# The value product of an attention kernel from fp32 to fp16 parts, with a new order of the copies around it

## The reference

```python
qh, kh, vh = split_heads(q @ Wq), split_heads(k @ Wk), split_heads(v @ Wv)
dots = einsum('bhid,bhjd->bhij', qh, kh) * SCALE          # then mask and causal mask
attn = softmax(dots)
out = einsum('bhij,bhjd->bhid', attn, vh)                 # the value product
x = x + tanh(g_xattn) * (out_as_rows @ Wo + bo)
```

## Time and profile before

| | before |
|---|---|
| median of 3 runs | 1624.48 us (1622.92 to 1630.77) |
| the profiled execution | 1626.47 us |
| its span, first to last instruction | 1624.6 us |
| busy share: PE, PEld, DVE, ACT, POOL | 94%, 77%, 85%, 77%, 64% |

### The profile page before, as it was taken

One profiled execution on the slowest core, in us unless ns is written; L12 is line 12 of the kernel. 1 busy time (PEld: TensorE's weight loads), 2 busy tenths in 40 slices (PEclk: granted clock), 3 DMA queues, 4 the chain that ended last, 5 costly groups with the idle time before them and its releaser, 6 DMA issues. The chain is left out here.

```text
span 1624.6 us, 38058 instructions
## 1 busy us (share of the span) xinstructions
PE 1530.6 (94%) x12556; PEld 1251.8 (77%) x12556; DVE 1385.1 (85%) x2247; ACT 1253.4 (77%) x3222; POOL 1033.8 (64%) x1004
## 2 busy tenths in 40 slices
PE   7899999999999999999999999789989997995998
PEld 5787887877877878878778788677767776775887
DVE  7888888888888888888888889878887998998996
ACT  5887887888778778878887787566758998885674
POOL 3988988888888889888888888600006664740000
PEclk9999999999999999999999999999998999997999
DMA  6554445444444544454444445369957884755664
GB/s 195 118 127 103 105 106 122 104 92 115 106 105 103 126 102 105 107 121 104 92 115 106 105 103 98 86 205 344 321 215 262 282 287 153 276 227 187 218 214 145
DMA packets 347365, 252.23 MB, mean 155 GB/s; under 512 B 287792, under 2 KB 317616, under 8 KB 344368
## 3 DMA queue, kind: packets, MB, share of 16 engines
q1 hardware_dynamic: 347312, 251.58, 55.1%
HBM read 105.25 MB, written 76.02 MB: 112 GB/s over the span
## 5 line engine op out<-in xcount | busy, mean ns | idle before, releaser
L496 ACT ACTIVATE prob<-masked,neg_max 128x128 f32<-128x128 f32 x1024 | 397.6, 391 | 35.1 <-DVE neg_max L662 31.6
L431 POOL TENSOR_TENSOR prob_parts<-prob,prob_parts 128x512 f16<-128x512 f32 x254 | 310.3, 1241 | 2.7 <-ACT prob_parts L504 1.6
L426 POOL TENSOR_TENSOR prob<-prob,scaled 128x512 f32<-128x512 f32 x256 | 271.6, 1061 | 20.1
L660 DVE TENSOR_TENSOR masked<-score,mask_add 128x512 f32<-128x512 f32 x256 | 174.6, 682 | 74.0 <-PE score L963 67.9
L504 ACT ACTIVATE prob_parts<-prob 128x512 f16<-128x512 f32 x254 | 159.0, 627 | 75.6 <-POOL prob L426 71.7
L496 ACT ACTIVATION_READ_ACCUMULATOR prob<-masked,neg_max 128x1 f32 x1024 | 193.3, 189 | 0.0
L662 DVE TENSOR_REDUCE neg_max<-masked 128x4 f32<-128x512 f32 x256 | 175.6, 686 | 8.8
L438 POOL TENSOR_TENSOR probT<-turn 128x512 f32<-128x512 f16 x125 | 173.2, 1386 | 0.0
L1723 POOL TENSOR_SCALAR xThi<-n_x 128x1024 fp32r<-128x1024 int16 x15 | 43.8, 2919 | 202.9 <-DMA n_x<-n_x_d 166.8
L976 PE MATMUL y<-wo_hi,o_hi 128*128 128x256 f32 x508 | 148.3, 292 | 15.9 <-DVE o_lo L667 15.2
L424 POOL TENSOR_TENSOR scaled<-rsums,pscale 128x4 f32<-128x4 f32 x256 | 66.4, 259 | 124.0 <-DVE rsums L654 123.9
(11 more groups left out here) (249 smaller groups left out, 4485.5 us busy)
## 6 DMA issues: line engine op xcount, KB each, us to landing
gate<-gate_d SPq DMA_DIRECT2D x30, 768.0 KB, 4.3
n_x<-n_x_d SPq DMA_DIRECT2D x25, 512.0 KB, 4.9
gate_d<-stage SPq DMA_DIRECT2D x8, 1536.0 KB, 5.5
n_u_d<-w_raw SPq DMA_DIRECT2D x16, 768.0 KB, 4.1
stage<-n_u_d SPq DMA_DIRECT2D x16, 768.0 KB, 6.0
gate_d<-gate SPq DMA_DIRECT2D x7, 1536.0 KB, 5.5
x_in<-in_x SPq DMA_DIRECT2D x16, 512.0 KB, 3.9
ctx_in<-in_ctx_columns SPq DMA_DIRECT2D x16, 512.0 KB, 4.8
```

The lines of the kernel that those rows point to most:

```text
L426: gp.tensor_tensor(prob[:, h], prob[:, h], scaled[:, h, :].rearrange("p (b o) -> p b o", o=1).broadcast_to([P, NB, P]), ALU.mult).then_inc ...
L431: gp.tensor_tensor(prob_parts[:, h, 1], prob[:, h].rearrange("p b k -> p (b k)"), prob_parts[:, h, 0], ALU.subtract).then_inc(prob_low, 1)
L496: nc.scalar.activation(prob[:, h, b, :], masked[:, h, b, :], ACT.Exp, bias=neg_max[:, h, b:b + 1], accum_out=psums[:, h, b:b + 1]).then_in ...
L660: nc.vector.tensor_tensor(masked[:, h], score[h][:], mask_add[:], ALU.add).then_inc(masked_done, 1)
```

## The change

- `times_v` multiplies fp16 parts: the turned high and low halves in `turn` are read directly, and the values are kept as fp16 high and low halves (`v16`). Three fp16 matmuls (high by high, high by low, low by high) take the place of one fp32 matmul. Both joins and `probT` go; the transposing DMA waits for `pv_done` instead of the join.
- So that fp16 holds them, the values are scaled by a bound for each group: the largest entries of the context by column (`ctx_top`, VectorE) times the largest entries of `Wv` by row (`w_top`, VectorE, once), summed by four one-column matmuls (`value_bound`, TensorE, in unit 7 for the next group) and turned into a factor (`value_scale`). The residual multiplies by `y_unit`, which undoes it.
- Each value product is copied twice: `values_high` on ScalarE, behind the copy of the keys, then `values` on VectorE (scaled product minus high half), behind the second reciprocals.
- TensorE takes the (first) value product of a unit right behind the keys, ahead of the `Wo` product.
- ScalarE's `high_prob` of the second head moves from the end of a unit to the next unit, behind the copy of the queries.
- Smaller moves: `add_bias` on GpSimd to unit 1, `residual`, `second_max` and `normalise` to other places of VectorE's units; at the start, the scores of unit 0 ahead of the values, and `w_high_part(3)` and the tanh into unit 0; the last unit is turned through an fp16 split.

```diff
-            def join_prob(u, h, slot, times):
-                dve.wait_ge(prob_turned[h][slot], 16 * times)
-                wait(dve, pv_done, u)
-                nc.vector.tensor_tensor(probT[:, h], turn[:, slot, h, 0:NB], turn[:, slot, h, NB:2 * NB],
-                                        ALU.add).then_inc(probT_copied[h], 1)
...
             def turn_prob(u, h):
                 sp.wait_ge(prob_low, 2 * u + h + 1)
-                wait(sp, probT_copied[h], u - 1)
+                wait(sp, pv_done, u - 1)
...
+            def values_high(g, i, n):
+                b, before = nth(g, i)
+                if n == 0:
+                    act.wait_ge(v_scaled, 4 * g + 3)
+                act.wait_ge(projected[b], before + 1)
+                nc.scalar.activation(v16[:, n % NB, n // NB, 0], proj[b][:], ACT.Copy, scale=v_mul[:, 0:1]).then_inc(v_high, 1)
...
+                if not isinstance(g, int) or 2 <= u < U + 2:
+                    high_prob(u - 2, 1, (c + 1) % 2, NC // 2 * g + (c - 1) // 2)
+                early = isinstance(g, int) and g == 0 and c < 3
...
                 if soft:
                     exps(u - 1, 0)
-                if new:
+                if new and not early:
                     copy_k(g, c, u)
+                for i, n in vs[:1]:
+                    values_high(g, i, n)
...
-            def values(g, c):
-                for i, n in jobs_of(c, "v"):
+            def values(g, jobs):
+                for i, n in jobs:
                     b, before = nth(g, i)
-                    dve.wait_ge(projected[b], before + 1)
-                    nc.vector.tensor_copy(v_sb[:, n % NB, 0:VH], proj[b][:]).then_inc(copied[b], 1)
+                    dve.wait_ge(v_high, NC * g + n + 1)
+                    nc.vector.scalar_tensor_tensor(v16[:, n % NB, n // NB, 1], proj[b][:], v_mul[:, 0:1], v16[:, n % NB, n // NB, 0],
+                                                   ALU.mult, ALU.subtract).then_inc(copied[b], 1)
+
+            def ctx_top(g):
+                dve.wait_ge(ctx_loaded, 16 * (g + 1))
+                nc.vector.tensor_reduce(c_top[:], ctx_in[:], X, ALU.max, apply_absolute_value=True).then_inc(v_scaled, 1)
...
             w_low_part(2)
+            nc.vector.tensor_reduce(w_top[:, 0], staged(2), X, ALU.max, apply_absolute_value=True)
+            dve.wait_ge(w_loaded[5], 16)
+            nc.vector.tensor_reduce(w_top[:, 1], staged(5), X, ALU.max, apply_absolute_value=True)
+            ctx_top(0)
             w_low_part(3)
...
+                    for n, (m, t) in enumerate(((0, 0), (0, 1), (1, 0))):
+                        for h in range(2):
+                            at = c % NB * P + h * HD
+                            last = nc.tensor.matmul(pv[h * HD:(h + 1) * HD, b, :], v16[:, b, c // NB, m, at:at + HD],
+                                                    turn[:, slot, h, t * NB + b, :], start=(n == 0), stop=(n == 2))
                 last.then_inc(pv_done, 1)
+
+            def value_bound(g):
+                pe.wait_ge(v_scaled, 4 * g + 1)
+                for k in range(KC):
+                    for half in range(2):
+                        last = nc.tensor.matmul(trans[:, 0, 0:1], c_top[:, k:k + 1].broadcast_to([P, P]), w_top[:, half, k:k + 1],
+                                                start=(k == 0 and half == 0), stop=(k == KC - 1 and half == 1))
+                last.then_inc(v_bound, 1)
...
+                if new:
+                    for i, n in jobs_of(c, "v")[:1]:
+                        value(g, i, n)
                 if oldest:
...
                     out_product(u - 4, (c - 4) % NC)
                 if nxt:
                     transpose_in(g, *ts[1])
+                    value_bound(g + 1)
```

More of the change, by code:

```diff
@@ L449, in step @@
                         make_rstd2(g - 1)
[L450 to L453, removed]
+                if c == 1 and not (isinstance(g, int) and g == 0):
+                    add_bias(g - 1)
+                if c == 6 and new and not more:
+                    add_bias(g)
                 if soft:
@@ L532, in step @@
                     exps(u - 1, 1)
-                if isinstance(g, int) and g == 0 and c < 3:
+                if early and c < 2:
                     w_high_part(4 + c)
-                if new and c > 2:
-                    for i, n in jobs_of(c, "v"):
-                        b, before = nth(g, i)
-                        act.wait_ge(projected[b], before + 1)
-                        nc.scalar.activation(v_sb[:, n % NB, VH:2 * VH], proj[b][:], ACT.Copy).then_inc(copied[b], 1)
+                for i, n in vs[1:]:
+                    values_high(g, i, n)
                 if soft:
@@ L731, in step @@
                     second_norm(g - 1, NB // 2, NB)
-                if c == 6 and more:
-                    normalise(g + 1)
+                if c == 5 and more:
+                    normalise(g + 1, 0, NB // 2)
+                if c == 6 and after_first and more:
+                    second_max(g - 1)
+                if c == 3 and after_first:
+                    residual(g)
                 if isinstance(g, int):
@@ L847, in _ @@
             attended_low(U - 3)
-            for h in range(2):
-                join_prob(U - 2, h, 0, U // 2)
             attended_low(U - 2)
             weight_values(2, 1)
[L852 to L855, removed]
+            for h in range(2):
+                dve.wait_ge(v_high, NC * G + h + 1)
+                nc.vector.tensor_tensor(turn[:, 1, h, NB:2 * NB], trans[:], turn[:, 1, h, 0:NB], ALU.subtract).then_inc(last_turned, 1)
+                if h == 0:
+                    ffn_low_part(0)
             for n in range(1, 4):
@@ L937, in scores_free, with times_v @@
                     wait(pe, masked_done, 2 * (u - 1) + h + 1)
-            def times_v(u, c, then=None):
+            def times_v(u, c, slot, times, then=None):
                 for h in range(2):
-                    pe.wait_ge(probT_copied[h], u + 1)
+                    if times is None:
+                        pe.wait_ge(last_turned, 2)
+                    else:
+                        pe.wait_ge(prob_turned[h][slot], 16 * times)
                 wait(pe, out_split, u)
@@ L996, in step @@
                     weights_left(g, c, jobs_of(c, "k")[0][0], 1)
+                if first:
+                    scores_free(g, c, u)
+                    scores(g, c, u)
+                    value_bound(0)
                 if nxt:
                     transpose_in(g, *ts[0])
+                if first or fourth:
+                    pe.wait_ge(w_ready, 3 if first else 6)
+                if new:
+                    for i, n in jobs_of(c, "v")[:1]:
+                        value(g, i, n)
                 if oldest:
@@ L1006, in step @@
                     transpose_in(g, *ts[1])
-                if first or fourth:
-                    pe.wait_ge(w_ready, 3 if first else 6)
+                    value_bound(g + 1)
                 if new:
-                    for i, n in jobs_of(c, "v"):
+                    for i, n in jobs_of(c, "v")[1:]:
                         value(g, i, n)
                 if old:
-                    times_v(u - 3, co, (g, c, u) if new else None)
-                if new:
+                    times_v(u - 3, co, (c + 1) % 2, NC // 2 * g + (c - 1) // 2, (g, c, u) if new else None)
+                if new and not first:
                     if not old:
```

122 lines of the change are left out of this document (71 added, 51 removed).

## The result

The changed kernel takes 1682.26 us (median of 4 runs, 1680.25 to 1685.06) against 1624.67 beside it: 1.034 times as long, interval 1.032 to 1.036. 1602 was forecast, with a range of 1586 to 1634. The profiled execution has a span of 1681.8 us, against 1624.6.

What follows compares the result with a forecast made beforehand. TensorE was taken to set the pace, 7.98 us a unit. Value product -24, order -23, value_bound +14, new stalls +6 and start +4.5 sum to -22.5 us: 1602 us from a 1624.48 median, range 1586 to 1634.

Steps and rivals of the forecast that it cites:

- The value product: TensorE's probabilities times values in fp16: 0.83 us instead of 1.03, 0.20 gained a unit, -24 us in all.
- Rival 2: Loads set the step of TensorE's value product, which then takes 1.17 us: 1644 us in all; chance 0.08.
- The order on TensorE: Value product ahead of the Wo product, second high half later on ScalarE: covers stalls, 1.55 us a group, -23 us.
- the stall of 0.82 and the refill: Unit 0's Wo product waiting for o_lo, with a 0.1 us pipeline refill: both claimed covered by the later Wo product.
- value_bound: Four one-column fp32 matmuls on TensorE in unit 7, once a group: 0.95 us each time, +14 us in all.
- The turned probabilities: Second head's later low half and transposing DMA on SyncE's queue: claimed hidden, as the deadline moves back further; no cost.
- the balance of the others: ScalarE, VectorE and GpSimd loads stay under TensorE's 7.8 us a unit; 0.4 us of new stalls a group, +6 us.
- the slack of the keys: Margin between the values' low half on VectorE and the next unit's keys on TensorE: 1.2 us in a clean unit.
- Rival 1: Vector chain becomes the bound, keys waiting for the values' low half: 0.88 us in four units, 1649 us; chance 0.10.
- The start: Reductions and value halves ahead of weight parts delay unit 1's keys to 27.2: +4.5 us, bounds 0 and +7.
- The tail: End of the attention: two VectorE joins go (-2.7), subtractions (+1.4) and second high half (0.6) come; taken as 0.
- the prediction's own drain of 0.23: Start and drain time c in the step model of TensorE's value product and scores: 0.23 us.

Runs made afterwards that it cites:

- e2: The changed kernel with VectorE's whole tail (residual, moments, norms, maxima) ahead of the second reciprocals instead of behind the values' low half: 1590.54 us, ratio 0.977.
- e1: The changed kernel with only the second layer norm's moments on VectorE moved ahead of the second reciprocals: 1643.47 us, ratio 1.009.
- e3: The changed kernel with GpSimd's low half of the probabilities cut from 512 columns to 32, order left alone: 1626.09 us, ratio 0.999.
- e4: The changed kernel with the values' low half ahead of the second reciprocals on VectorE, the tail right behind these: 1618.67 us, ratio 0.995.
- e6: e2 with w_high_part(4) on ScalarE and w_low_part(4) on VectorE brought forward at the start: 1588.37 us, ratio 0.976.
- e9: e6 with the values' low half ahead of the second reciprocals in the first group alone: 1591.35 us, ratio 0.978.
- e8: e2 without the two reductions of Wv at the start and the wait for its second half, a constant in their place: 1591.1 us, ratio 0.978.

## Why the prediction was wrong

**The value product: right.** 0.83 forecast, 0.79 measured; as the mean of units 1 to 4 it is 0.23 less than before, and 125 times 0.23 is -29 us, not -24. Rival 2 fell, for which `pv` would have taken 1.17. By the 81 ns of the Trainium skill (TensorE: Matmul & The Clock Gate, "Back-to-back issue gap") `pv` would be 1.20 us by estimate, and the trace disagrees for these pairs of 64-column loads.

**The order on TensorE: right on the old stalls.** Unit 0 is 1.17 us shorter, 0.23 of it by `pv`: the stall of 0.82 and the refill are gone. With the tail early (e2) a group wins 63.81 - 60.97 = 2.84 us; 8 x 0.23 for `pv` and -0.88 for `value_bound` leave 1.88 for the order, 1.55 forecast.

**`value_bound`: right**, 0.88 (483.55 to 484.43) against 0.95. The turned probabilities were hidden, as forecast: no engine waits for them or for SyncE from 200 to 1000 us.

**The failed step is the balance of the others: "I allow 0.4 us of new stalls a group: +6 us".** It is 5.6 us a group: 66.56 less e2's 60.97. Over fifteen groups that is some 84 us, and it decides the sign. Three things were wrong in it. The waiter: I measured the slack of the keys (1.2 us), but behind the low half and the tail come the mask, the maxima and `o_lo`, which the `Wo` product needs. The size of the tail: I took it at 1.5 us of VectorE by itself, where in units 5 and 6 it takes 4.30 and, on average, 3.90 us from the reciprocal to the mask with the low half (0.75); in e1 the low half alone stands there in unit 5, and the stretch is 0.77. And the lateness of the second reciprocals: 0.4 us forecast, 1.85 measured for unit 5 (0.18 us behind its start, 1.67 ahead of it before). These add up: `o_lo` ends 6.49 us after the start of unit 5, before 3.01; 1.85 + 1.62 (4.30 less the 2.68 of before) is 3.47. The `Wo` product itself moved back by the values' 1.36, and unit 5 had lost 0.31 before: 3.47 + 0.31 - 1.36 = 2.4 us of new wait. The trace has unit 5 of this group at 9.74, 2.40 over the clean 7.34, and 2.17 of it as idle time ahead of the `Wo` product. e1, e3 and e4 show that the block is the cause, each from another side (the tail's place, GpSimd's length, the low half's place). e2 shows that the lateness of the reciprocals alone isn't: there they come 0.48 us behind the start of unit 6, and unit 6 takes 7.39.

The Trainium skill (SBUF — State Buffer, "SBUF: two separate sides") says that VectorE and GpSimd share a port pair, an exclusive lock held for a whole instruction, so that a VectorE operation with two SBUF inputs blocks fully against a GpSimd operation that reads SBUF. The trace agrees: 0.16 us become 1.14, and the low half, which reads PSUM and one tile of SBUF, stays at 0.75. The trace of before had it in view (1.03 and 1.09 for two of the moments, rows under e4); I read the durations by groups and missed it.

**Rival 1 named the right chain and the wrong end**: keys waiting for the low half, 0.88 us in four units, 1649. Its tail was the cause, its price took no account of GpSimd's block.

**The clock was no term of mine.** Full in the attention of the kernel before, it falls after the stalls of the changed one. The windows of TensorE's granted clock (last but two), in unit 6 of the changed kernel:

```profile
474.00:475.00 1.00, 1.00 (x6) 1.00 (x6) 0.96 (x4) 1.00 (x5) 0.00 (x0) 0.50 0.96 383
475.00:476.00 1.00, 1.00 (x7) 1.00 (x6) 0.58 (x2) 1.00 (x5) 0.89 (x2) 0.50 0.15 57
```

TensorE's timeline in that unit:

```profile
473.61 0.58 PE L1033 MATMUL y<-wo_hi,o_hi 128*128 128x256 f32 x1 [2.44 <-DVE o_lo L680]
...
476.47 0.71 PE L999 MATMUL pv<-turn,v 128*64 128x128 f16 x18
```

The start:

```profile
19.00:23.00 4.00, 4.00 (x13) 3.26 (x13) 2.24 (x5) 0.57 (x1) 0.00 (x0) 0.57 0.32 81
...
27.00:31.00 4.00, 2.95 (x10) 2.37 (x11) 3.56 (x5) 1.09 (x4) 0.00 (x0) 0.80 0.31 112
31.00:35.00 4.00, 4.00 (x42) 2.60 (x40) 1.74 (x7) 3.57 (x16) 1.26 (x3) 0.78 0.00 0
```

0.50 is 1.2 GHz. In unit 6, behind waits of 2.17 and 2.44 us in two units, the `Wo` product takes 2.86 us (473.61 to 476.47) instead of 1.51. The clock isn't what made the group longer: the groups from 152.97 and 685.18 hold no stretch at half clock and take 66.84 and 66.86 us, against a mean of 66.53.

**The start: mis-sized.** Keys of unit 1 at 28.05 (before 22.94), 27.2 forecast; but the first group loses 9.25 us, not 4.5 (7 at most); with the tail early (e2) it is 6.6. Units 0 to 3 lose 6.4: 1.49 us of waiting for `c_top` ahead of `value_bound`, and in the three windows above, by estimate, up to 4 x (0.43 + 0.20 + 0.22) = 3.4 us to the half clock, where before all of 15 to 35 us ran at 1.00. Units 4 to 7 lose 2.9, most of it in unit 6 (10.35 against 7.81), the tail again (8.03 in e2). In e6 the keys still wait for the low half twice, 1.39 and 2.30 us; in e9, 0.58 and 1.44. How the rest divides stays open: e8, without the reductions of `Wv`, starts 0.6 us later and its first group is 2.1 us shorter than e2's, and its time isn't lower.

**The end of the attention ("The tail" of the prediction): 0 forecast, 0.3 measured.** From the start of the last unit to the end of the last `Wo` product it takes 24.5 us, before 24.2. The 6.0 us of the last group stand ahead of that: its units 4 to 6 lose 8.3 (12.95 in unit 6 against 7.63), its units 0 to 3 win 2.2. With VectorE's tail early (e2) units 4 to 6 take 7.34 to 7.67, so these are the same stalls. The other 3.2 us of the span lie in the feed-forward layer and aren't shown to be the change's: the same code takes 571.6 us there in e2 and 577.0 in e9.

## What to carry to other kernels

Before adding an operation to a queue, follow what stands behind it on that queue to the last waiter, and take the durations that those have at their new place in time, not their mean. Where GpSimd works from SBUF, short VectorE operations on SBUF tiles belong ahead of the event that starts GpSimd, and operations that read PSUM can stand behind it. A change that loses may hold a gain: here the same new steps, with the tail in another place, are 2.3% faster than the kernel before.

## What the runs showed of the hardware

Operations of 0.16 us on four columns lasted up to 1.14 us when they met a GpSimd operation, to its end (within 0.02 us in the changed kernel's rows). A `TENSOR_SCALAR` with a single SBUF tensor is held too (`v_eps` 1.03 us in e4); three `BATCH_NORM_STATS2` of one SBUF tile aren't (0.41 us each in e2, from 485.81, beside GpSimd's product from 485.90 to 486.94). TensorE's clock was at half from 473.1 to 476.5, behind two waits of 2.17 and 2.44 us in two units, and in the next group from 531.2 to 534.6, behind one of 2.17; e2, without such waits, has 1.00 from 200 to 900 us. An fp16 step of `pv`, a pair of 64-column loads and 128-column passes, costs (0.79 - 0.23) / 12 = 0.047 us, an estimate with the prediction's own drain of 0.23.
